# A decoder layer's cross-attention scores: the copies of steps and sums go to GpSimd, the eviction of finished outputs goes to ScalarE

## The reference

```python
# x: 1024 tokens (layer-normed), cond: 2048 context rows; 16 heads of 32
q = fq_sym((x @ Wq + bq) / sqrt(32), axis=-1)      # 8-bit steps per token and head
k = fq_sym(cond @ Wk + bk, axis=-1)
v = fq_sym(cond @ Wv + bv, axis=keys)
attn = softmax(q @ k.T)                            # all 1024 queries x all 2048 keys, per head
s = max(attn, axis=-1) / 255                       # 8-bit, unsigned
attn = clip(round(attn / s), 0, 255) * s
out = attn @ v
return out @ Wp + bp
```

## Time and profile before

| | |
|---|---|
| median of 3 runs | 1165.16 us (1164.48 to 1166.69) |
| the profiled execution's own time | 1169.33 us |
| its span, first instruction to last | 1167.6 us |
| mean granted TensorE clock | 0.972 of full speed |
| busy in the span: PE, DVE, ACT, POOL | 965.9, 821.3, 645.2, 322.5 us (83, 70, 55, 28%) |
| the stage of the edit | about 360.5 to 829.6 us |
| GpSimd's code configuration in that stage (a queue instruction, 11 ns) | at 360.6 us |
| GpSimd's waits for VectorE's eviction | 6, together 308.3 us |

### The profile page before, as it was taken

One profiled execution on the slowest core, in us unless ns is written; L12 is line 12 of the kernel. 1 busy time (PEld: TensorE's weight loads), 2 busy tenths in 40 slices (PEclk: granted clock), 3 DMA queues, 4 the chain that ended last, 5 costly groups with the idle time before them and its releaser, 6 DMA issues. The chain is left out here.

```text
span 1167.6 us, 21732 instructions
## 1 busy us (share of the span) xinstructions
PE 965.9 (83%) x8017; PEld 660.7 (57%) x8017; DVE 821.3 (70%) x1389; ACT 645.2 (55%) x1040; POOL 322.5 (28%) x310
## 2 busy tenths in 40 slices
PE   4988989899896767676777776767799899999996
PEld 3754745788683444444444444444678665655665
DVE  6747746899898999999999999999554321111217
ACT  3454243455478878888888888888434112212221
POOL 1225035466613970101010101010464400000014
PEclk9999999899997999999999999999899899999999
DMA  8400001311000030000000000000021693132216
GB/s 312 182 1 1 1 1 37 109 36 36 10 1 1 2 127 2 0 0 0 0 0 0 0 0 0 0 0 0 3 77 39 249 403 134 62 126 64 63 49 204
DMA packets 24857, 68.18 MB, mean 58 GB/s; under 512 B 2722, under 2 KB 6818, under 8 KB 23778
## 3 DMA queue, kind: packets, MB, share of 16 engines
q1 hardware_dynamic: 20114, 52.48, 12.2%
q0 software_dynamic: 4400, 14.42, 3.9%
q10 hardware_dynamic: 288, 0.52, 0.1%
HBM read 49.07 MB, written 18.35 MB: 58 GB/s over the span
## 5 line engine op out<-in xcount | busy, mean ns | idle before, releaser
L1333 ACT ACTIVATE cs_p_int<-cs_s_b,cs_bias,cs_step_now 128x1024 int16<-128x1024 f32 x128 | 154.2, 1204 | 64.5 <-DVE cs_bias L1368 64.4
L1361 DVE TENSOR_REDUCE cs_top<-cs_s_b 128x1 f32<-128x512 f32 x256 | 164.9, 686 | 12.7 <-PE cs_s_b L1390 3.5
L1390 PE MATMUL cs_s_b<-k_parts,q_int 96*128 96x512 bf16 x256 | 79.4, 392 | 112.1 <-ACT cs_p_int L1333 112.0
L1398 PE MATMUL cs_tp<-ident,cs_p_int 128*128 128x128 f16 x2048 | 158.8, 221 | 3.2 <-ACT cs_pT L1339 1.1
L1349 DVE TENSOR_REDUCE cs_top<-cs_s_a 128x1 f32<-128x1024 f32 x128 | 155.5, 1215 | 4.3 <-PE cs_s_a L1390 4.3
L1333 ACT ACTIVATE cs_p_int<-cs_s_a,cs_bias,cs_step_now 128x1024 int16<-128x1024 f32 x128 | 152.8, 1194 | 0.0
L1398 PEld LDWEIGHTS cs_tp<-ident,cs_p_int 128*128 128x128 f16 x2048 | 121.3, 98 | 48.1 <-issue 44.3
L2237 PE MATMUL ff_h<-ff_experts,ff_zgT 128*128 x368 | 112.9, 460 | 0.9 <-ACT ff_zgT L1776 0.9
L1390 PE MATMUL cs_s_a<-k_parts,q_int 96*128 96x512 bf16 x256 | 79.9, 395 | 22.3 <-ACT cs_p_int L1333 18.0
L1390 PEld LDWEIGHTS cs_s_b<-k_parts,q_int 96*128 (+1 forms) x256 | 14.8, 98 | 135.0 <-ACT cs_p_int L1333 126.6
L1376 DVE COPY cs_pT<-cs_tp 128x1024 int16<-128x1024 int16 x128 | 87.2, 681 | 3.2 <-PE cs_tp L1398 3.1
(11 more groups left out here) (309 smaller groups left out, 2146.2 us busy)
## 6 DMA issues: line engine op xcount, KB each, us to landing
ff_experts<-in_experts_dram SPq DMA_DIRECT2D x8, 2176.0 KB, 12.4
slots<-sa_zero SPq DMA_DIRECT2D x1, 5888.0 KB, 24.9
ff_zg<-slots POOLq DMA_DIRECT2D x23, 256.0 KB, 2.9
run_y<-ff_yv SPq DMA_DIRECT2D x23, 256.0 KB, 2.0
ff_raw<-in_weights_dram SPq DMA_DIRECT2D x6, 768.0 KB, 5.4
ck_raw<-in_ctxT_dram SPq DMA_DIRECT2D x8, 512.0 KB, 3.5
stage<-in_cwkv_dram SPq DMA_DIRECT2D x2, 1024.0 KB, 5.0
out_dram<-x_res SPq DMA_DIRECT2D x8, 256.0 KB, 2.1
```

The source lines that it names most:

```text
L1333: nc.scalar.activation(p_int[:, u, half * HALF:(half + 1) * HALF], s[:, :], ACT.Exp, bias=bias[:, u:u + 1], scale=step_now[:, h:h + 1], ac ...
L1361: nc.vector.tensor_reduce(top[:, u, 1 + c:2 + c], s_b[:, c * 512:(c + 1) * 512], AX_X, ALU.max).then_inc(max_ok, 1)
L1390: ins = nc.tensor.matmul(s[:, c * 512:(c + 1) * 512], q_int[0:3 * D, t, h, :], k_parts[0:3 * D, h, keys:keys + 512], start=True, stop=True)
L1398: ins = nc.tensor.transpose(tp[:, k, :], p_int[:, u, key:key + P].bitcast(F16), ident16[:, :])
```

## The change

The names `act_tile` and `dve_tile` go; three semaphores take their place. GpSimd now copies the steps, the negative steps and the sums, in halves of eight heads: `next_low(t)` for heads 0 to 7 once the tile before has done eight heads, `next_high(t)` for heads 8 to 15 once it has done sixteen. ScalarE and VectorE wait for the low half at head 0 and for the high half at head 8. ScalarE evicts `out` at the second unit, after the unit's two exponentials and ahead of its copy of transposed integers. The last tile's sums are copied by GpSimd at the end.

```diff
         @block.gpsimd
         def _(pool):
+            def steps_of(t, heads, ready):
+                nc.gpsimd.tensor_copy(step_now[:, heads], q_step[:, t, heads]).then_inc(ready, 1)
+                nc.gpsimd.tensor_copy(nstep_now[:, heads], q_nstep[:, t, heads]).then_inc(ready, 1)
+
+            def sums_of(t, heads, ready):
+                nc.gpsimd.tensor_copy(z_sum[:, t, heads, :], z_now[:, heads, :]).then_inc(ready, 1)
+
+            def next_low(t):
+                pool.wait_ge(ea_ok, (t - 1) * H + HH)
+                steps_of(t, slice(0, HH), low_heads)
+                sums_of(t - 1, slice(0, HH), low_heads)
+
+            def next_high(t):
+                pool.wait_ge(ea_ok, t * H)
+                steps_of(t, slice(HH, H), high_heads)
+                sums_of(t - 1, slice(HH, H), high_heads)
+
+            steps_of(0, slice(0, HH), low_heads)
+            steps_of(0, slice(HH, H), high_heads)
             for h in range(H):
+                if h == H - 2:
+                    next_low(1)
                 of_head = v_raw[:, :, h * D:(h + 1) * D]
...
+            next_high(1)
             pool.wait_ge(w_in, 32)
             nc.gpsimd.tensor_copy(w_hi[:, :, :], w_raw).then_inc(whi_ok, 1)
...
             for t in range(TT - 1):
-                pool.wait_ge(act_tile, 2 * t + 2)
+                if t:
+                    next_high(t + 1)
+                pool.wait_ge(low_heads, 2 + 3 * (t + 1))
+                pool.wait_ge(high_heads, 2 + 3 * (t + 1))
                 pool.wait_ge(out_read, t + 1)
                 scale_output(nc, pool, t, scaled, 5 * t, o_raw, z_sum, p_step, v_step, minus_one)
+                if t + 2 < TT:
+                    next_low(t + 2)
             pool.wait_ge(scaled, 5 * (TT - 1))
+            pool.wait_ge(ea_ok, UNITS)
+            sums_of(TT - 1, slice(0, H), sums_kept)
+            pool.wait_ge(sums_kept, 1)
...
         @block.scalar
         def _(act):
-            def keep_sums(t, n):
-                act.wait_ge(ea_ok, n)
-                nc.scalar.copy(z_sum[:, t, :, :], z_now[:, :, :]).then_inc(act_tile, 1)
-                act.wait_ge(act_tile, 2 * t + 2)
+            def keep_outputs(t, n):
+                act.wait_ge(av_ok, n - 1)
+                nc.scalar.mul(o_raw[:, t - 1, :], out[:, :], P_UNIT).then_inc(out_read, 1)
 
             def step(t, h, n):
                 if not exists(n):
+                    if h == 1:
+                        keep_outputs(t, n)
                     return
                 u = h % 2
                 if h == 0:
-                    if at_least(n, H):
-                        keep_sums(t - 1, n)
-                    nc.scalar.copy(step_now[:, :], q_step[:, t, :]).then_inc(act_tile, 1)
-                    act.wait_ge(act_tile, 2 * t + 1)
+                    act.wait_ge(low_heads, 3 * t + 2)
+                if h == HH:
+                    act.wait_ge(high_heads, 3 * t + 2)
...
+                if h == 1 and at_least(n, H):
+                    keep_outputs(t, n)
                 act.wait_ge(tb_ok, n + 1)
...
-            keep_sums(TT - 1, UNITS)
...
                     if h == 0:
-                        if at_least(n, H):
-                            v_.wait_ge(bias_ok, n)
-                        nc.vector.tensor_copy(nstep_now[:, :], q_nstep[:, t, :]).then_inc(dve_tile, 1)
-                        v_.wait_ge(dve_tile, t + 1)
+                        v_.wait_ge(low_heads, 3 * t + 2)
+                    if h == HH:
+                        v_.wait_ge(high_heads, 3 * t + 2)
...
-                if h == 1 and at_least(n, H):
-
-                    v_.wait_ge(av_ok, n - 1)
-                    nc.vector.tensor_scalar(o_raw[:, t - 1, :], out[:, :], P_UNIT, None, ALU.mult).then_inc(out_read, 1)
```

More of the change, by code:

```diff
@@ L1246, in cross_scores @@
         top_ok = sem("top_ok")
-        act_tile = sem("act_tile")
-        dve_tile = sem("dve_tile")
+        low_heads = sem("low_heads")
+        high_heads = sem("high_heads")
+        sums_kept = sem("sums_kept")
         w_in = sem("w_in")
@@ L1283, in _ @@
                 sp.dma_start(ff_raw[:, c, :], ff_dram[c, :, :]).then_inc(ff_in[c], 16)
+        HH = H // 2
         @block.gpsimd
         def _(pool):
+            def steps_of(t, heads, ready):
[13 more added lines that the diff above has]
+            steps_of(0, slice(HH, H), high_heads)
             for h in range(H):
+                if h == H - 2:
+                    next_low(1)
                 of_head = v_raw[:, :, h * D:(h + 1) * D]
```

## The result

| | before | changed |
|---|---|---|
| median of the runs made together | 1164.82 us (4 runs, 1162.65 to 1166.69) | 1156.20 us (4 runs, 1155.90 to 1157.80) |
| ratio | | 0.9927, 95% interval 0.9910 to 0.9945 |
| the profiled execution: own time, span | 1169.33, 1167.6 us | 1155.91, 1154.2 us |
| first bias to last bias (units 0 to 127) | 459.05 us | 452.88 us |
| rest of the span | 708.6 us | 701.3 us |

The kernel became faster by 0.73%, 8.6 us, where 5.8 were forecast; the time forecast, 1159.4, is 3.2 too high, and 1156.2 lies under the lower end of the range, 1157.5. The last two rows split the span at the stage of the edit: its loop gained 6.17 us, and the rest, whose code is the same, shows 7.3 less (7.2 before rounding). These two are taken up one after the other.

What follows compares the result with a forecast made beforehand. The stage was taken as bound by the loop bias, exponential, scores, maxima, beside a nearly full VectorE; 2.8 + 2.4 + 0.2 + 0.35 = 5.8 us off 1165.16 gave 1159.4, range 1157.5 to 1163.0 (8 in 10).

Steps and rivals of the forecast that it cites:

- What bounds the stage: Cross-attention scores: the loop bias, exponential, scores, maxima sets the period, 3.54 us a unit, with VectorE nearly full.
- Ordinary changes of tile: Six tile changes, t = 2 to 7: VectorE's eviction costs 0.42 and its negative-steps copy 0.05 each; gain 2.8 us.
- The 0.09 of the register wait: Interval before the eviction's: exponential starts late behind a register instruction, 0.09 us above steady, left in after the change.
- The first change of tile: VectorE's copy held under GpSimd's subtraction, then TensorE at low clock: three intervals 13.23 become 10.79, gain 2.4 us.
- VectorE has nothing left that was seen to be held: First tile change: GpSimd's subtraction moves to about 421.5, but no copy remains on VectorE to stall; underlies the 2.4.
- Start: Stage start: VectorE's first copy goes, maxima at 362.77 instead of 362.97, gain 0.2 us if GpSimd's copies are done.
- Low-clock spells: At 606 and 664 us, after evictions, TensorE was slow for a unit; gain between 0 and 0.7, 0.35 taken.
- The eviction on ScalarE: Eviction takes 0.50 of ScalarE's 0.58 us free per unit, 0.08 to spare; cost taken as nothing, at most 0.8.
- the last step: Stages around untouched, so the gain is taken off the three-run median: 1165.16 - 5.8 = 1159.4 us.
- the eviction on ScalarE's path: Rival: ScalarE's eviction does not hide at tile changes; 1162.9 us if none hides, 1161.2 if half; chance 0.11.
- The wait for code: Rival at stage start: GpSimd's first copies wait for code, costing 5.0 us, time 1164.4 or later; chance 0.08.
- The stall: Rival at first tile change: the stall moves to another VectorE instruction, losing the 2.4, time 1161.8; chance 0.08.

Runs made afterwards that it cites:

- experiment 12: Changed kernel with the order of waits turned on ScalarE and VectorE only inside the loop, where counts come from registers: 1153.20 us, 0.9921 of before.
- experiments 5 to 7: Changed kernel plus, on VectorE, the negative-steps copy at head 0, an extra copy at head 1, or a maximum at head 1: 1158.67, 1162.06, 1158.17 us.
- (8): Changed kernel with the eviction made twice on ScalarE, the first time into a buffer that nothing reads: 1160.96 us.
- (9): Changed kernel with GpSimd's first four copies moved behind its first multiplication of the values and its code configuration: 1163.56 us.
- (6): Changed kernel with an extra VectorE copy of 128x16, SBUF to SBUF, at head 1 of each tile: 1162.06 us, stage 457.62.

## Why the prediction was right, and where it was wrong

**What bounds the stage** was right: 3.54 a unit in both kernels, and most of the stage's gain came from the changes of tile: 5.3 of the 6.17 in the first pair of profiles. Of the others, 0.4 is the low-clock spells below, and 0.5 is spread over the steady units, 3.544 on average against 3.540; in the second profile of the kernel before they are 3.541.

**Ordinary changes of tile:** 3.96 became 3.54 and 3.67 became 3.62, six times: 2.8, as forecast. The 0.09 of the register wait stayed, as forecast, and experiment 12 took it away.

**The first change of tile:** 13.23 became 10.78, 2.4 as forecast. Its cause, a copy held under GpSimd's instruction, is shown by experiments 5 to 7. "VectorE has nothing left that was seen to be held" decided it: the moved subtraction lies beside VectorE's unit 17, and one copy of 16 columns left there would have cost 4.7 (457.62 - 452.88) and turned most of the gain back. That its size was 1.49 was luck of one phase; in the second profile of before it was 1.79 and the three intervals 5.29, 3.84, 4.61, by which this change of tile gained 3.0.

**Start:** 0.2, and measured 0.21 (2.86 to 2.65 from the first maximum to the first bias).

**Low-clock spells:** 0.35 taken for less idle time without the eviction, and this step has nothing for it. The two long units (0.69) are gone in the changed kernel, but they are gone in the second profile of the kernel before too, which at its six later turns has 3.54 in every interval behind the eviction's: they belonged to one execution, not to the eviction. Against that, units 7, 8 and 25 are 0.07, 0.05 and 0.15 longer than steady in all three profiles of the changed kernel, 0.27 that the sum left out, at a granted clock of 1.00 in the first of them (385 to 393 and 448 to 455 us). At head 8, where the wait for the upper heads was added, the exponential starts 0.09 after the bias's end; for unit 25 the runs show no cause.

**The eviction on ScalarE:** nothing, as forecast; the spare time was 0.18, not 0.08. A piece costs 0.48 of ScalarE's time, not 0.50, and the eviction starts sooner than the copy whose place it takes: 2.37 after the unit's first exponential (478.85 to 481.22), where the copy starts 2.49 after it in the earlier trace rows (467.36 to 469.85).

The sum for the stage, 2.8 + 2.4 + 0.35 = 5.55 from first to last bias, stands against 6.17 in the first pair of profiles and 5.8 between the means of all (458.8 of two, 452.95 of three). That it comes so near is in part luck: the first change of tile gives 2.4 or 3.0 by the profile, the spells 0.7 or nothing, and the 0.27 wasn't seen.

**What failed** is the last step, "the stages around are untouched, so I take the difference over: 1165.16 - 5.8 = 1159.4", with its range, "a little below the forecast for scatter". The difference was right for the stage; what failed is the claim that the other 700 us can be taken over from three runs, for this level was not known to 2 us. Three runs gave 1165.16; 57 later ones gave 1161.8, and 1161.8 - 5.8 = 1156.0, against 1156.6, the median of the changed kernel's 16 runs in three sessions. I had read the scatter from the three runs (0.7 below, 1.5 above), and the profiled execution itself stood 4.2 above them: the profile held a warning that the rest of the program varies by more, and the range should have reached 3 to 4 us below the forecast. Why the first four runs of the kernel before lie higher than most later ones stays open; with it, so does why the difference came out as 8.6 there and 5.0 and 4.3 later.

The rivals: the eviction on ScalarE's path did not come, but stood 0.18 us away (8). The wait for code did not come, and would have cost 6.8 (9); it was priced at 5.0, and 6 to 8 with a second load. The stall did not move to another instruction, and with a copy left in unit 17 would have cost 4.7 (6), not 2.4.

## What to carry to other kernels

A stall of one engine's small instruction under another engine's long one is priced by the phase between them, from nothing to the whole long instruction: ask what is left in that stretch after the change, not what it cost in one trace. Split a profile at the edited stage and compare several executions: the stage here repeats within 0.5 us, the rest of the same program within 10, so forecast a difference from the stage, and give the level the scatter of the rest. A stretch at a low clock in one profile is no cost of the code beside it until a second profile shows it again. At the turn of a loop, look which wait the last instruction ahead of the critical one carries; turning two waits was worth 1.7 us, this whole change about 6.

## What was not expected of the hardware

- VectorE's copy of 128x16 from SBUF to SBUF took 4.31 us under a GpSimd subtraction of 4.51, while the copy of transposes from PSUM (128x1024, 0.68) and the reductions kept their lengths under the same subtraction in the changed kernel (419.47 to 423.99).
- After 4.78 us of idle TensorE, its granted clock in 426 to 430 us was 0.50 (the lower level, 1.2 GHz), and two matrix products of the scores took 1.03 instead of 0.60. Two profiles of one program differed by 9.7 us outside the stage, with such stretches in different places.
- GpSimd's copies of 128x8 took 0.19 us each and ran before its code configuration; the first multiplication behind it started 6.97 us after the last copy.
